# Graph attention on one core: TensorE takes its words and two quarters of the older products earlier in a round, ScalarE prepares the sums before the lookup rows

## What is computed

```python
def gat_conv(x, src, dst, W, att_src, att_dst, bias, n_nodes):
    h = (x @ W).reshape(n_nodes, Hh, Cc)
    a_src = (h * att_src).sum(-1)
    a_dst = (h * att_dst).sum(-1)
    alpha = leaky_relu(a_src[src] + a_dst[dst])
    m = jax.ops.segment_max(alpha, dst, num_segments=n_nodes)
    e = jnp.exp(alpha - m[dst])
    denom = jax.ops.segment_sum(e, dst, num_segments=n_nodes)
    w = e / jnp.clip(denom, 1e-16)[dst]
    out = jax.ops.segment_sum(w[:, :, None] * h[src], dst, num_segments=n_nodes)
    return out.reshape(n_nodes, Hh * Cc) + bias
...
x = _layernorm(x + _L0_gnn_ref(x, edge_index, ...), axis=-1)
x = _layernorm(x + _L1_gnn_ref(x, src, dst, ...), axis=-1)
```

## Time and profile before

| | before |
|---|---|
| median of 3 runs | 6752.11 us |
| lowest, highest | 6746.11, 6760.09 us |
| the profiled execution, its time | 6752.08 us |
| its span from first to last instruction | 6750.3 us |
| busy TensorE, VectorE, ScalarE, GpSimd | 4987.2, 4543.9, 2986.8, 4612.2 us |
| mean granted TensorE clock | 0.767 of full |

### The profile page before, as it was taken

One profiled execution on the slowest core, in us unless ns is written; L12 is line 12 of the kernel. 1 busy time (PEld: TensorE's weight loads), 2 busy tenths in 40 slices (PEclk: granted clock), 3 DMA queues, 4 the chain that ended last, 5 costly groups with the idle time before them and its releaser, 6 DMA issues. The chain is left out here.

```text
span 6750.3 us, 105201 instructions
## 1 busy us (share of the span) xinstructions
PE 4987.2 (74%) x21652; PEld 3760.2 (56%) x21653; DVE 4543.9 (67%) x13212; ACT 2986.8 (44%) x4940; POOL 4612.2 (68%) x4838
## 2 busy tenths in 40 slices
PE   6777777777777577777777777757777777777776
PEld 5555555555555455555555555535555555555553
DVE  6666666666666667777777777766666666666668
ACT  3344444444344245555555555534344444333435
POOL 2777777777777477777777777737777777777754
PEclk8777777777777677877777777767778777777777
DMA  7555555555555355555555555535555555555545
GB/s 266 144 150 147 148 147 145 149 148 148 147 146 149 98 149 157 159 159 159 157 160 156 158 160 158 155 109 154 152 151 154 153 152 150 150 152 153 154 126 153
DMA packets 505818, 1026.49 MB, mean 152 GB/s; under 512 B 146891, under 2 KB 313199, under 8 KB 504878
## 3 DMA queue, kind: packets, MB, share of 16 engines
q0 software_dynamic: 226208, 633.50, 35.1%
q1 hardware_dynamic: 278798, 382.44, 17.5%
HBM read 931.37 MB, written 84.15 MB: 150 GB/s over the span
## 5 line engine op out<-in xcount | busy, mean ns | idle before, releaser
L1036 POOL DMA_INDIRECT e_rows<-table,loaded x4689 | 4515.6, 963 | 1960.9 <-issue 1694.8
L1293 PE MATMUL e_p_mm<-e_rows,e_onehot 128*128 128x264 f32 x9378 | 2851.9, 467 | 10.5 <-DVE e_rows L1477 7.5
L1293 PEld LDWEIGHTS e_p_mm<-e_rows,e_onehot 128*128 128x128 f32 x9378 | 2177.1, 237 | 493.0 <-issue 11.6
L1477 DVE TENSOR_TENSOR e_rows<-e_rows,e_p_pair 128x1024 f32<-128x1024 f32 x1173 | 1414.0, 1205 | 0.0
L1705 DVE TENSOR_TENSOR_SCAN e_fwd<-e_mask,e_p_one 64x128 f32<-64x128 bf16 (+1 forms) x294 | 121.8, 414 | 1797.1 <-PE e_p_one L1376 1795.3
L1469 DVE TENSOR_TENSOR e_onehot<-e_col,e_p_pair 128x512 f32<-128x512 f32 (+1 forms) x1176 | 903.3, 768 | 79.5 <-issue 75.2
L1301 PE MATMUL e_p_one<-ad_parts,e_onehotT 128*128 x5586 | 707.6, 189 | 154.7 <-issue 146.0
L1301 PEld LDWEIGHTS e_p_one<-ad_parts,e_onehotT 128*128 128x128 bf16 x5586 | 555.7, 103 | 331.7 <-issue 203.8
L1155 ACT ACTIVATE e_onehotT<-e_onehotT,minus_pidx 128x2432 bf16<-128x2432 bf16 x294 | 681.6, 2319 | 42.2 <-DMA e_pass<-pass_rows 41.8
L1158 ACT ACTIVATE e_onehotT<-e_onehotT,one_col 128x2432 bf16<-128x2432 bf16 x294 | 682.7, 2322 | 9.6
L1388 PE MATMUL e_p_small<-ident,e_fwd 64*1 64x64 f32 (+1 forms) x294 | 77.0, 262 | 588.2 <-issue 580.8
(11 more groups left out here) (327 smaller groups left out, 6006.6 us busy)
## 6 DMA issues: line engine op xcount, KB each, us to landing
e_onehotT<-rel_rows SPq DMA_DIRECT2D x294, 608.0 KB
e_rows<-table,loaded POOLq DMA_INDIRECT x4689
e_own_row<-table SPq DMA_DIRECT2D x196, 128.0 KB, 3.1
table<-e_rows_out SPq DMA_DIRECT2D x98, 132.0 KB, 2.0
table<-n_rows_out SPq DMA_DIRECT2D x14, 910.0 KB, 15.5
table<-e_rows_out SPq DMA_DIRECT2D x98, 130.0 KB, 2.6
n_inputs<-in_x_turned SPq DMA_DIRECT2D x14, 896.0 KB, 11.5
e_mask<-mask_rows SPq DMA_DIRECT2D x196, 64.0 KB
```

What stands on the lines that cost most here:

```text
L1036: pool.indirect_dma_start(rows[k][:, g, 0:TW], None, table[L], bass.IndirectOffsetOnAxis(ap=idx[k][:, g:g + 1], axis=0)).then_inc(s_gat[k] ...
L1293: ins = nc.tensor.matmul(p_mm[:, bass.ds(region, MW)], onehot[:, g, :], rows[k][:, g, :], start=False, stop=True, skip_group_check=True)
L1477: return nc.vector.tensor_tensor(feats, feats, p_e[:, gs, :].unsqueeze(3).to_broadcast([P, n, H, C]), ALU.mult)
```

## The change

On TensorE, `offs`, `flag` with `extra_ad` and `slots` are loaded together with `regions`, ahead of the wait for the scores, and `old_slots` only behind `products(2)`. `products(0)` moves ahead of the carried columns and `products(1)` ahead of the tops; the wait for `cleared` moves along, ahead of `products(0)`. On ScalarE, `prepare_sums` moves ahead of `lookup_rows`. In layer 1, one over the square root is no longer made by a Sqrt on ScalarE and a reciprocal on VectorE, but on ScalarE alone as exp(-0.5 ln(v + eps)), and one activation table set is asked for at the start of the edge phase's ScalarE list.

```diff
--- before.py
+++ after.py
@@ -1130,6 +1130,7 @@
             @block.scalar
             def _(act):
                 zero_col = iota_d[:, 0:1]
+                nc.scalar.preload_act_table_set("natural_log_exp_and_others")
 
                 banks = p_mm[:].rearrange("p (r n) -> p r n", n=BANK)
 
@@ -1172,7 +1173,9 @@
                 def roots(j, r):
 
                     act.wait_ge(s["mean"], j)
-                    nc.scalar.activation(root[:, r:r + 1], mv[:, r, 1:2], ACT.Sqrt, bias=eps_col[:, 0:1]).then_inc(s["root"], 1)
+                    nc.scalar.activation(root[:, r:r + 1], mv[:, r, 1:2], ACT.Ln, bias=eps_col[:, 0:1]).then_inc(s["root"], 1)
+                    act.wait_ge(s["root"], j)
+                    nc.scalar.activation(rinv[:, r:r + 1], root[:, r:r + 1], ACT.Exp, scale=-0.5).then_inc(s["rinv"], 1)
 
                 def normalise(j, r):
 
@@ -1235,10 +1238,10 @@
                         nc.scalar.copy(summed[:], p_node[:, 0:D]).then_inc(st["kept"], 1)
                     if NORMED and finished(w, 6):
                         roots(place_of(act, w, 6), (u - 6) % TURNS)
+                    if not first:
+                        prepare_sums(old, past)
                     if not (isinstance(w, int) and w == WINDOWS - 1):
                         lookup_rows((u + 1) % TURNS, used(u, i, TURNS, -1), count(act, now + 1))
-                    if not first:
-                        prepare_sums(old, past)
                     if CARRY:
                         carried(w, u, i)
                     act.wait_ge(st["gap"], now)
@@ -1366,7 +1369,9 @@
                     now, past = ago(0), ago(1)
                     if not first:
                         regions = words(pe, REGION_ROW, (w - 1) * G, G, (REGIONS - 1) * BANK)
-                        old_slots = words(pe, WINDOW_ROW, (w - 1) * WIN + W_TILE, EXTRAS, G - 1)
+                    offs = words(pe, AD_ROW, w * G, G, (PLACES - 1) * ADS_W)
+                    flag, *extra_ad = words(pe, WINDOW_ROW, w * WIN + W_FLAG, 1 + EXTRAS, (PLACES - 1) * ADS_W)
+                    slots = words(pe, WINDOW_ROW, w * WIN + W_TILE, EXTRAS, G - 1)
                     def products(q):
                         if not first:
                             for g in range(4 * q, 4 * q + 4):
@@ -1379,9 +1384,6 @@
                         add_linear(w, past)
                     if CARRY and finished(w, 7):
                         multiply(w, u)
-                    offs = words(pe, AD_ROW, w * G, G, (PLACES - 1) * ADS_W)
-                    flag, *extra_ad = words(pe, WINDOW_ROW, w * WIN + W_FLAG, 1 + EXTRAS, (PLACES - 1) * ADS_W)
-                    slots = words(pe, WINDOW_ROW, w * WIN + W_TILE, EXTRAS, G - 1)
                     wait_apart(pe, st["scan"], now)
                     wait_apart(pe, st["factor"], past)
                     for dst, col, o in ((0, fwd[:, P - 1:P], 0), (1, bwd[:, 0:1], P)):
@@ -1394,20 +1396,22 @@
                     for e in range(EXTRAS):
                         last = lookup(two, G + e, bass.ds(slots[e] * (3 * H), 3 * H), extra_ad[e])
                     last.then_inc(st["lookup"], 1)
+                    if not first:
+                        wait_apart(pe, st["cleared"], past)
+                    products(0)
                     wait_apart(pe, st["carry"], now)
                     for o, src in ((COLS_AT, outf), (COLS_AT + 1, outb)):
                         last = nc.tensor.transpose(p_small[0:HG, o:o + 1], flat(src), ident[0:1, 0:1])
                     last.then_inc(st["colsum"], 1)
-                    if not first:
-                        wait_apart(pe, st["cleared"], past)
+                    products(1)
                     wait_apart(pe, st["top"], now)
                     nc.tensor.transpose(p_top[:, 0:HG], seg[:], ident[0:HG, 0:HG]).then_inc(st["topT"], 1)
-                    products(0)
-                    products(1)
                     if CARRY and finished(w, 6):
                         wait_apart(pe, st["topread"], now)
                         turn(w, u)
                     products(2)
+                    if not first:
+                        old_slots = words(pe, WINDOW_ROW, (w - 1) * WIN + W_TILE, EXTRAS, G - 1)
                     wait_apart(pe, st["fdist"], now)
                     nc.tensor.matmul(p_small[:, MAT_AT:MAT_AT + H], first_row[:], fdiff[:], start=True, stop=True
                                      ).then_inc(st["fmat"], 1)
@@ -1605,8 +1609,6 @@
                 def shifts(w, u):
 
                     j, r = place_of(dve, w, 6), (u - 6) % TURNS
-                    dve.wait_ge(s["root"], j)
-                    nc.vector.reciprocal(rinv[:, r:r + 1], root[:, r:r + 1]).then_inc(s["rinv"], 1)
                     dve.wait_ge(s["rinv"], j)
                     nc.vector.scalar_tensor_tensor(shift[:, r:r + 1], mv[:, r, 0:1], -1.0, rinv[:, r:r + 1], ALU.mult, ALU.mult
                                                    ).then_inc(s["shift"], 1)
```

## The result

| | before | after |
|---|---|---|
| median | 6752.36 us (5 runs) | 6688.94 us (5 runs) |
| lowest, highest | 6746.11, 6760.09 us | 6681.28, 6708.81 us |
| ratio of the times, 95% interval | | 0.9911, 0.9892 to 0.9929 |
| the profiled execution, its time and span | 6752.08, 6750.3 us | 6686.26, 6684.4 us |
| mean granted TensorE clock | 0.767 | 0.816 |

The change makes the kernel 0.9% faster, by 63 us. I had forecast 160 us. The sign is right and the time lies in the range, but six tenths of the gain are missing.

A forecast was written before the change was run, and what follows sets the result against it. GpSimd's waits for TensorE's extras bound the kernel: 1.45 us less per two-round loop is 0.72 us per round, 213 us in 294 rounds; three quarters, 160 us, gives 6592 us, with about 85% within 6510 to 6725.

The forecast's parts named there:

- the price of the words: TensorE ahead of the scores' transpose: 1.5 to 2.5 us of added loads, mostly hidden in idle time, cost 0.2 us.
- The rest of the chain: TensorE, scores' transpose to extras: earlier lookups and quarters 0 and 1 bring the extras 1.4 us earlier; 1.45 us used.
- The carried columns: TensorE behind quarter 0: columns come 1.7 us later, so msg3's 3.1 us of slack ahead of the extras falls to nothing.
- The loop of two rounds: GpSimd gather, landing, scores, TensorE extras: 42.2 us for two rounds, so a microsecond saved gives half per round.
- three quarters: Share taken of the 213 us gain, as GpSimd doesn't wait in some rounds: 160 us.
- A: TensorE's clock stays at 0.50 through quarters 1 and 2 and the extras: 7140 us; chance 8%.
- B: Clock returns 7 us into the products, or late words delay the scores' transpose 1.5 us: 6730 us; chance 12%.
- D: Shorter waits for extras, but the gather's landing grows from 2.3 to 3 us: 6690 us; chance 10%.
- C: Scores to extras shrinks by 2 us or more, GpSimd's own issue becomes the bound: 6510 us; chance 15%.
- Covers that held: Table loads, cleared, later one-hot passes and SyncE's loads cost no time; old_slots hidden by 1.8 us of queued products.
- Signs named ahead: Profile signs of a right forecast, among them GpSimd's waits under 80 us, clock near 0.77, extras about 17 us behind scores.
- The sign for "wrong": A clock below 0.7, or a longer time from scores to the scans with the loads in front of them.

The follow-up runs named there:

- the words alone: Kernel before with only the word loads moved (offs, flag with extra_ad and slots ahead of the scores' transpose, old_slots behind products(2)): 6836.48 us, ratio 1.0141.
- the last experiments: Whole change with carried columns ahead of quarter 0 and tops ahead of quarter 1, 6517.02 us; the same with region words loaded behind the lookups, 6515.37 us.
- the columns first: Whole change with carried columns kept ahead of quarter 0 and tops between quarters 0 and 1; also called the fastest but one: 6517.02 us, ratio 0.9661 to before.
- the fifth load: Whole change plus a second, really read load of the 16 region words ahead of the scores' transpose: 7008.24 us, ratio 1.04 to the kernel before.

## Why the prediction was wrong by 97 us

**The step that failed is the price of the words**: "That is hidden in a round like the example, and costs up to 1.5 us where TensorE is late. I take 0.2 us." It measured 1.19 us in the mean of all rounds. The sum didn't even hold the 0.2 us: it gave 1.4 us without them and 1.2 with them, and took 1.45. The added 1.5 to 2.5 us were right (4.3 less 2.3 us, 2.0). Wrong was the cover. I counted 1.85 us of idle matmul side ahead of the transpose and some part of the last quarter. But the rest of the change makes faster rounds, which bring the next scores sooner, and `msg3`, now without slack, lets the queue run ahead of the products by less (by the records of loads and products, the first load begins 3.5 us ahead of the end of the last product in the example of before, and 2.5 us in that of after; the medians of the run are 3.6 and 2.5 us). So the example's idle time was not there any more when the loads came. Not all of the 1.19 us is due to the words: the words alone delay the transpose by 0.83 us, with the first load 3.6 us ahead of the end of the products as before; the rest of the change without them delays it by 0.63 us, with the first load 2.5 us ahead. The prediction had nothing for the second. As an estimate, with 0.2 us in place of 1.19, and all else as measured, the extras would come 1.84 us earlier; less the 0.32 us of landing, half of it in 294 rounds is 223 us. No run shows that kernel, and part of the gain would fall on rounds in which GpSimd doesn't wait.

**The rest of the chain was a little better than forecast.** From transpose to extras I had 1.45 us, measured 2.03. So 1.45 + 0.58 - 1.19 gives the 0.85 us that the extras come earlier behind the scores. The clock was given back 3.1 us into quarter 0 in the example (0.65 in the second stretch is 0.5 up to 3196.7 and 1.0 from there), where it had taken 3.7 us before; the stretches of the kernel after, PEclk in the third last column:

```profile
3193.60:3195.60 2.00, 1.97 (x5) 1.56 (x6) 1.97 (x5) 1.97 (x2) 1.39 (x3) 0.50 0.81 121
3195.60:3197.20 1.60, 1.60 (x7) 1.05 (x5) 0.57 (x3) 1.60 (x2) 1.29 (x2) 0.65 0.77 304
3197.20:3199.30 2.10, 2.10 (x11) 1.54 (x11) 1.93 (x5) 0.67 (x3) 1.49 (x3) 1.00 0.68 245
```

**The carried columns** came 1.39 us later behind the transpose, and 2.58 us later behind the scores, where I had 1.7; what lies between the two is the late transpose again. That this place was worth repairing, as the last experiments show, the forecast had in hand ("This is the price"), and it didn't ask what the other order would give.

**The loop of two rounds** held: half of the extras' gain arrives. I took three quarters of it on top, for rounds in which GpSimd does not wait. The measured 66 us of span are 85% of the 78 us. This factor was not far off. What it left out is the second loop, of one round, on TensorE, which the kernel before runs with 1.36 us of slack at its head and the kernel after with none: 0.9% is what is left when a change gives 2.03 us to one loop and takes the slack of the other.

**The rivals.** A (the clock does not come back, 8%) fell: the granted clock rose from 0.767 to 0.816. The Trainium skill ("TensorE: Matmul & The Clock Gate", A second HAM failure mode: psum-queue depth-cycling) tells of a kernel in which micro-idles between groups of matmuls make the clock go back and forth. Taken as a rule, as the forecast took it, it speaks for a lower clock in the split block; this trace shows the contrary. B (12%) named the right mechanism, "if late words push the scores' transpose by 1.5 us in most rounds", with a price of 1.5 us beside a measured 1.19, and gave 6730 us. I had held it for a special case. D (10%), a longer landing, is there with 0.32 us of the 0.7 us that I allowed. C (15%), GpSimd as the bound, did not come with this change, but with the columns first.

**Covers that held.** The table loads at L1175 are gone, `cleared` and the passes over the one-hot matrix wait for nothing new, `old_slots` behind `products(2)` costs nothing that shows. One wait is new and was not in the forecast: TensorE waits 52.2 us in 93 rounds ahead of quarter 2, nearly all in layer 2, for VectorE's `msg2`. I had taken layer 2 as the others.

**Signs named ahead.** Of eight, five came (the columns without "issue", `cleared` no releaser, VectorE waiting for the columns, TensorE at L1360 and L1288, no table load); three did not: GpSimd's waits 177.6 us in place of under 80, the clock 0.816 in place of 0.77, the extras 18.6 us behind the scores in place of 17. The sign for "wrong", a longer time from scores to scans, came.

## What to carry to other kernels

An idle stretch in front of a wait is cover only as long as the wait is as late as it was: price work that is moved there against the round as the change leaves it, and look for every loop that runs through the place, with how many rounds each takes, since a microsecond costs all of itself in a loop of one round and half in one of two. Parts of a change in a cyclic schedule don't add: here two parts that lose 1.4% and 3.0% by themselves win 0.9% together. When a change moves bulk work ahead of short steps, ask of each step who on another engine continues from it, and leave those in front of the bulk: the transposes of the columns and of the tops, 0.2 to 0.3 us each, moved back ahead of one quarter of the products each, were worth more than the change.

## What was unexpected on the hardware

Loads of words into TensorE's registers are dear: 1.29 and 1.11 us for the two of 16 words in the kernel after (medians; up to 1.79), 0.51 for four and 0.78 for three, each in series in the queue, where the profile shows only idle time by "issue"; 5.9 us for five of them in the example. The granted clock rose to 0.816 when the block of products was split, and was 0.801 in the kernel with the fifth load, though TensorE's idle time ahead of the transpose had grown to 3.74 us in the example; it was 0.775 in the fastest but one. Here clock and speed went opposite ways, so the mean clock was no guide to the time. The late transposes gather behind the turn of the hardware loop: in the kernel before, the first round of each six has it 2.3 to 2.8 us behind the scores (means of the three layers), the others 0.6 to 1.2; in the kernel after the first two have 3.3 to 4.7 us, the others 0.8 to 1.8. Why the first round of a turn is late was not tried.
